# Units of 32 rows in two threads half a unit apart, layer 0 from squares of field sums, MLP in three chunks

## What is computed

```python
# e: (1024, 32, 16) = rows of 32 tables picked by ids
xk = x0 = e
for W in (W0, W1, W2):                     # W0: (32, 32, 64), W1 and W2: (32, 64, 64)
    xk = relu(einsum('bmd,bhd,mhk->bkd', x0, xk, W))
    outs.append(sum(xk, axis=2))           # 64 features of each layer
h = concatenate([concatenate(outs, 1), dense_ctx], 1)        # 208 features
h = maximum(h @ W_top1 + b_top1, 0); h = maximum(h @ W_top2 + b_top2, 0)
y = h @ W_top3
```

## Time and profile before

| | us |
|---|---|
| median of 3 runs (671.03 to 674.77) | 673.65 |
| the profiled execution | 669.01 |
| its span, first to last instruction | 667.2 |

### The profile page before, as it was taken

The page is one execution under the profiler, slowest core; times in us unless marked ns, Lnnn a source line. Parts: engine busy times, 40 slices in busy tenths (PEclk is TensorE's granted clock), DMA queues, the critical chain, the costliest instruction groups (busy, mean ns, idle before and its releaser), DMA issues.

```text
span 667.2 us, 7015 instructions
## 1 busy us (share of the span) xinstructions
PE 588.9 (88%) x2524; PEld 184.4 (28%) x2524; DVE 560.8 (84%) x419; ACT 235.8 (35%) x401; POOL 486.1 (73%) x364
## 2 busy tenths in 40 slices
PE   2558898989899997989899998989898998999998
PEld 1512232222222232322232222323222222323333
DVE  0048998999898998989899998999899989989620
ACT  1030707152441607153341607061432517070513
POOL 6776487877878787877878787887878787858420
PEclk9989898999999898999999999999999999999999
DMA  4398895968869494968969494959779594956000
GB/s 109 95 386 270 325 368 185 344 248 286 332 197 387 146 371 165 353 240 272 346 187 392 162 379 171 365 202 334 286 237 381 167 394 164 397 181 239 0 0 1
DMA packets 82709, 167.95 MB, mean 252 GB/s; under 512 B 38177, under 2 KB 43297, under 8 KB 82674
## 3 DMA queue, kind: packets, MB, share of 16 engines
q1 hardware_dynamic: 74482, 165.39, 68.9%
q0 software_dynamic: 8192, 2.11, 2.3%
HBM read 164.05 MB, written 3.41 MB: 251 GB/s over the span
## 4 chain that ended last, share of the span: by engine, by line
DMA 41%; DVE 18%; SPq 14%; PE 13%; issue 7%; POOL 5%; ACT 2%; ACTq 0%; DVEq 0%
DMA x_rot<-x_rows 20%; DMA x_rows<-gathered 15%; SPq L261 13%; DVE dve_ring L498 10%; PE acc L588 8%; DVE l_tiles L528 5%; POOL gathered L358 4%; DMA x_wide<-x_rows 4%; DVE z_half L512 2%; PE x_ps L613 2%; ACT x_rot_ps L407 2%; SPq L252 1%; DMA gathered<-in_table,idx 1%; PE x_rot_ps L606 1%; PE x_rot_ps L607 1%
## 5 line engine op out<-in xcount | busy, mean ns | idle before, releaser
L498 DVE TENSOR_TENSOR dve_ring<-x_wide,x_ps 128x1024 f32<-128x1024 f32 (+1 forms) x329 | 460.6, 1475 | 11.2 <-ACT x_ps L422 11.2
L588 PE MATMUL acc<-dve_ring,w_sb 128*64 128x512 f32 x1640 | 385.0, 599 | 17.1 <-DVE dve_ring L498 16.2
L383 POOL TENSOR_TENSOR pool_ring<-x_wide,x_sb 128x1024 f32<-128x1024 f32 x102 | 241.7, 2378 | 78.0 <-PE acc L588 45.1
L358 POOL DMA_INDIRECT gathered<-in_table,idx x256 | 243.2, 950 | 72.1 <-issue 69.5
L588 PEld LDWEIGHTS acc<-dve_ring,w_sb 128*64 128x64 f32 x1640 | 110.7, 137 | 275.1 <-issue 147.7
L560 PE MATMUL acc<-l_tiles,w_sb 128*64 128x512 f32 x256 | 76.0, 696 | 37.0 <-DVE l_tiles L528 36.1
L588 PE MATMUL acc<-pool_ring,w_sb 128*64 128x512 f32 x408 | 104.8, 592 | 0.0
L407 ACT COPY x_rot_ps<-x_rot 128x1024 f32<-128x1024 f32 x16 | 16.3, 1016 | 209.5 <-DMA x_rot<-x_rows 209.5
L422 ACT ACTIVATE x_ps<-acc 64x512 f32<-64x512 f32 x128 | 73.1, 571 | 38.7 <-PE acc L564 22.5
L528 DVE TENSOR_TENSOR l_tiles<-x_wide,x_rot_ps 128x1024 f32<-128x1024 f32 x32 | 38.8, 1218 | 56.2 <-ACT x_rot_ps L407 29.2
L431 ACT COPY x_sb<-layer_out 64x512 f32<-64x512 f32 x128 | 79.0, 617 | 3.4
(11 more groups left out here) (28 smaller groups left out, 54.6 us busy)
## 6 DMA issues: line engine op xcount, KB each, us to landing
x_wide<-x_rows SPq DMA_DIRECT2D x256, 512.0 KB, 11.8
l_tiles<-x_rows SPq DMA_DIRECT2D x32, 512.0 KB, 9.3
x_rot<-x_rows SPq DMA_DIRECT2D x16, 512.0 KB
gathered<-in_table,idx POOLq DMA_INDIRECT x256, 2.3
x_rows<-gathered SPq DMA_DIRECT2D x15, 128.0 KB
x_rows<-gathered SPq DMA_DIRECT2D x15, 80.0 KB
w_sb<-in_w SPq DMA_DIRECT2D x2, 512.0 KB, 3.7
x_wide<-in_W_top SPq DMA_DIRECT2D x1, 512.0 KB, 6.7
```

The source lines that it names most:

```text
L358: pool.indirect_dma_start(gathered[:, p % 2, i * DIM:(i + 1) * DIM], None, table, bass.IndirectOffsetOnAxis(ap=idx[:, p, i:i + 1], axis=0) ...
L383: nc.gpsimd.tensor_tensor(pool_ring[:, slot, :], x0_step(p, layer, t), x_sb[layer - 1][:], ALU.mult).then_inc(pool_made, 1)
L498: nc.vector.tensor_tensor(dve_ring[:, slot:slot + width, :], x0_step(p, layer, t, width).rearrange("p (s n) -> p s n", n=WIDE), x_ps[layer ...
L588: last = nc.tensor.matmul(a[c * HK:(c + 1) * HK, :], w_sb[layer - 1][:, step_at(layer, t), :], tile[:, c * CHUNK:(c + 1) * CHUNK], start=( ...
```

## The change

A unit is now 32 rows, 512 columns. There are 32 of them in two threads: thread `c` has units (c, 0) to (c, 15) and owns output half `c` of PE, of `acc[j % 2]` and of `layer_out`. Five functions write each engine's order down from slots. A unit takes 37: layer 1 in slots 0 to 15, layer 0 of the thread's next unit in 16 to 20, layer 2 in 21 to 36. Thread 1 begins 16 slots behind thread 0. So PE's pair of matmuls in a slot is one of each thread, mostly in different layers.

Layer 0 changes its arithmetic. For a pair of fields 2ab = (a+b)^2 - a^2 - b^2. Per unit four matmuls of 32 input rows and 128 outputs (`sums`, L603) sum pairs of fields into four PSUM banks, one matmul on each 32 rows of the array. ACT squares the sums in two instructions of 1,024 columns (L480, L482) and the fields in one of 512 (L484). PE contracts four tiles of squares (L615) and the fields' own (L617), whose weights are corrected once at the start. DVE has no part in it any more, and `x0_rot`, `l0_tiles` and their loads are gone.

DVE works on doubles (two steps of 512 columns, the 1,024 of a step before) or two doubles at once; POOL on doubles, 84 in all in place of 102 steps. `finish` writes half as many columns per unit. There are 512 step loads of 256 KB in place of 304 loads of 512 KB, and 8 gathers per unit. The MLP takes chunks of 512, 384 and 128 rows; the first two stand between the last units' steps on PE, and each has its own output DMA.

```diff
+THREADS = 2
+ROWS = 32
+UNITS = BATCH // (THREADS * ROWS)
+UNIT_SLOTS = 2 * STEPS + L0_STEPS
+DELTA = 16
+L2_SLOT = STEPS + L0_STEPS
+LEAD = 6
+MLP_CHUNKS = ((0, 512), (512, 384), (896, 128))
...
+def pool_doubles(c, j, layer):
+    if j == 0 and layer == 1:
+        return ()
+    if j + AHEAD >= UNITS:
+        return {1: (3, 6), 2: (3, 7)}[layer]
+    return {1: (6,), 2: ((3, 7), (5,))[c]}[layer]
...
+def pe_order():
...
+            works += [(at + i, "step", c, j, 1, i) for i in range(STEPS)]
+            works += [(at + L2_SLOT + i, "step", c, j, 2, i) for i in range(STEPS)]
...
+            works.append((sum_slot(c, j) + 0.5, "sums", c, j + 1, 0, 0))
+            works += [(l0_slot(c, j) + i, "layer0", c, j + 1, 0, i) for i in range(L0_STEPS)]
...
+        works += [(at + i - LEAD, "product", c, j, 1, i, width) for i, width in dve_groups(c, j, 1)]
+        works += [(max(at + L2_SLOT + i - LEAD, at + STEPS + 2.5 + i / 100), "product", c, j, 2, i, width)
...
-            for p in range(PAIRS):
-                contract(p, 1)
-                if p + 1 < PAIRS:
-                    layer0(p + 1)
...
+            def sums(c, j):
+                n = sum_number(c, j)
+                wait_first_step(pe, c, j)
+                if n:
+                    pe.wait_ge(squares_made, 3 * n)
...
+                for q in range(SUM_TILES):
+                    to = x_ps[:, bank + q, :] if q < 2 else sums_ps[:, q - 2, :]
+                    rows = slice(q * FIELDS, (q + 1) * FIELDS)
+                    nc.tensor.matmul(to, in_pair_sb[rows, :], x0_step(c, j, 1, 0)[rows, :],
+                                     start=True, stop=True).then_inc(sums_made, 1)
...
+            def squares(c, j):
+                n = sum_number(c, j)
+                act.wait_ge(sums_made, 4 * (n + 1))
...
+                nc.scalar.activation(pair_squares[:, c, 2:4, :], sums_ps[:], ACT.Square).then_inc(squares_made, 1)
+                wait_first_step(act, c, j)
+                nc.scalar.activation(own_squares[:, c, :], x0_step(c, j, 1, 0), ACT.Square,
```

More of the change, by code:

```diff
@@ L67, in l0_order @@
[L67 to L88, removed]
@@ L91, in ring_slot, with begin, sum_slot @@
-def ring_slot(steps, ring, p, layer, i):
-    return (made_before(steps, p, layer) + i) % ring
-def dve_groups(p, layer):
-    groups = []
[L97 to L100, removed]
+def begin(c, j):
+    return DELTA * c + UNIT_SLOTS * j
+def sum_slot(c, j):
+    if j < 0:
+        return begin(c, 0) - 6
+    return begin(c, j) + (4 if j > 0 else (20, 10)[c])
@@ new lines, in z_slot, with act_order @@
+def z_slot(layer, tile):
+    j = 2 * tile + 1
+    return {0: evac0_slot(1, j - 1) + 4, 1: begin(1, j) + STEPS + 5, 2: begin(1, j + 1) + 2}[layer]
+def act_order():
+    works = []
+    for c, j in [(c, -1) for c in range(THREADS)] + units():
+        at = begin(c, j)
+        if j >= 0:
+            works.append((at + STEPS, "finish", 1, c, j))
+            works.append((at + UNIT_SLOTS, "finish", 2, c, j))
+        if j + 1 < UNITS:
+            works.append((sum_slot(c, j) + 1.5, "squares", 0, c, j + 1))
+            works.append((evac0_slot(c, j), "finish", 0, c, j + 1))
+    works += [(z_slot(layer, tile) + 1, "place", layer, tile, 0) for layer in range(LAYERS) for tile in range(TILES)]
+    for n, first in enumerate((begin(0, UNITS - 1) + STEPS, begin(1, UNITS - 1) + STEPS, begin(1, UNITS) + 3.5)):
+        works += [(first + 1.5 * i + 1.7, "mlp", n, i, 0) for i in range(len(MLP_PARTS))]
+    return in_order(works)
@@ new lines, in sp_order @@
+def sp_order():
+    works = []
+    for c, j in units():
+        at = begin(c, j)
+        if j + 1 < UNITS:
+            works.append((at + 22, "block", c, j + 1, 2))
+            works.append((at + 26, "block", c, j + 1, 3))
+        if j + 2 < UNITS:
+            works.append((at + 28, "stage", c, j + 2, 0))
+            works.append((at + 30, "block", c, j + 2, 0))
+            works.append((at + 34, "block", c, j + 2, 1))
+    works.append((begin(1, UNITS - 2) + UNIT_SLOTS, "mlp", 0, 0, 0))
+    return in_order(works)
@@ L145, in cin_tower @@
[L145 to L151, removed]
+        acc = [psum(f"acc{i}", [P, COLS]) for i in range(2)]
+        sums_ps = psum("sums_ps", [P, 2, COLS])
+        x_ps = psum("x_ps", [P, 4, COLS])
@@ L216, in block_slot @@
[L216 to L231, removed]
@@ L246, in _ @@
         def _(sp):
[L247 to L257, removed]
@@ L419, in finish @@
                 if layer < 2:
[L420 to L423 removed]
+                    for half in range(2):
+                        nc.scalar.activation(x_ps[out_half(half), BANK[layer + 1, c], :], a[out_half(c), :],
+                                             ACT.Relu).then_inc(x_ps_made[layer + 1][c], 1)
```

785 lines of the change are left out of this document (396 added, 389 removed).

## The result

| kernel | median us (range) | ratio to before, 95% | profiled span |
|---|---|---|---|
| before | 673.36 (671.03 to 674.77) | 1 | 667.2 |
| changed | 1536.98 (1535.81 to 1538.12) | 2.291 (2.2815 to 2.3005) | 1536.3 |

The forecast was 654 us, its range 643 to 696. The kernel is slower, and by far more than any rival allowed.

A forecast was written before the change was run, and what follows sets the result against it. DVE was taken to bound the kernel before, PE after the change. Start 64, middle 494.2 (period 34.6), last units 77.4 and tail 12 make 647.6 us of span; with 6.4 to the median 654 us, range 643 to 696.

The forecast's parts named there:

- the paragraph on DMA: Step loads: 512 of 256 KB for 304 of 512 KB, issued 11 or more slots before use; nothing counted.
- 159.8 + 14.28 * P: Whole kernel's time in us for a period P, one unit of each thread; forecast P 34.6 us.
- late loads: Rival at each `sums`: staging and block 0 come 2 us late, all of PE waits; P = 38, 702 us; chance 0.06.
- Work counts: DVE's instructions counted from the order: about 515 us busy in all, products no longer than 1.2 and 2.3 us.
- Price of sums: PE's two new blocks per period: four matmuls side by side 0.86 us, splits 0.35, so 1.2 us a block; period 34.1.
- serial sums: Rival on PE: the four matmuls of `sums` run one after another, 3.43 + 0.35 us a block; 721 us; chance 0.07.
- strict order: Rival on PE: no matmul starts before the one written ahead; 2.9 us a block, P = 37.5, 695 us; chance 0.10.
- Joints, 0.5 us: Handovers between PE, ACT and DVE around layer 0: mostly covered by stock, 0.5 us added per period, making 34.6 us.
- the two engines hold each other up: Rival: DVE waits for PE's ring slots, PE for products; PE gets 95%, P = 35.9, 672 us; chance 0.15.
- Start: Start of the kernel: first product at 31.2 us, 15 us sooner, and slot 26 ends at 64 us.
- Last units and tail: End of the kernel: last units 77.4 us by PE with MLP chunks between steps, then a tail of 12 us.
- From span to median, 6.4 us: Added to the forecast span of 647.6 us, as the median of the runs lies 6.4 us over the profiled span.

The follow-up runs named there:

- e1: Changed kernel with the two outer dimensions of the step loads' source exchanged (32 fields outermost, then 4 quarters), weights reordered to match; 695.32 us, ratio 1.034.
- e11: e9 with one load for each block of four steps, 128 partitions of 8 KB, in place of four of 2 KB; 649.23 us, ratio 0.966.
- e5: e1 with all of DVE's products two steps wide, none of four; 664.11 us, ratio 0.989.
- e15: e11 with DVE's products of four steps put back; 684.49 us, ratio 1.020.
- e9: e5 with the MLP's weights loaded 10.5 slots earlier; 660.26 us, ratio 0.981.

## Where the prediction failed

**The step that failed is the paragraph on DMA**: "The share of 0.77 to 0.79 may stay, with smaller rows at a worse rate" and "I count nothing here". I read sizes and counts of the loads, and not the order of the dimensions in `load_step`. What I put at nothing cost 842 us of the 883 between forecast and result, by e1. With the order of the dimensions read, the rows give the price: 276 GB/s at a share of 0.79 are 21.8 for each engine, four engines move 87 GB/s, and a period loads 32 * 0.262 = 8.4 MB: 96 us. With 159.8 + 14.28 * P that is 1,531 us. That this comes so near to 1,537 is luck: the period was 90.2 us, which gives 1,448, and the start and the end, which the formula keeps as they were, took some 90 us more. The rival "late loads" named the right place and the right victim (SP serves two threads in one line, PE's wait blocks both), but it was priced as a delay of 2 us, not as a rate.

The other steps are read from e1 and e11, where the loads are spread:

- *Work counts*: right. DVE 516.3 us for 515 in the changed kernel; products last 1.21 and 2.29 us as before.
- *Price of sums*: right. The passes start at 214.31, 214.84, and in e11 a period without any wait is 34.20 us, for 34.1 by count. A block costs 1.17 us for 1.2 (in e11 204.13 to 205.73 from the last pass start before it to the first behind it, less 0.43); 0.31 of that is the change of split, where my own rows add up to 0.3 and I wrote 0.35. Four matmuls on different input rows run side by side; serial sums and strict order fall.
- *Joints, 0.5 us*: the term that was too small. e1's period is 36.8 for 34.6. From slot 26 to slot 555 (the first step behind the last layer 0 product) it took 528.5 us (71.7 to 600.2) for 494.2: 34.3 us too much. I had seen the two engines hold each other up as a rival at P = 35.9 and chance 0.15; once the loads are spread it was the true case, and stronger. I weighed it by how full the engines are; what decided was how long one instruction waits and works (four slots, 2.3 us) with another thread's need behind it. e5 removes most of it (34.9), e15 with the loads in time brings it back (36.6). What e5 and e9 have over 34.20 is gone in e11, together with PE's waits for loads.
- *Start*: slot 26 at 71.7 us in e1 and 68.8 in e11, for 64. In e1 the first product comes at 33.1 us for 31.2, and behind it DVE waits three times for ring slots, 2.2 to 3.4 us, which I hadn't counted.
- *Last units and tail*: 93.9 us in e1 for 89.4, with a wait of 3.63 us for the MLP's weights, which I had not looked for; 85.7 in e11.
- *From span to median, 6.4 us*: too large. In e11 the median lies 2.0 us over the span. The profiled execution of the kernel before was faster than each of its other runs (669.01 us, the others 671.03 and more).

In e11 the errors of the parts cancel, which is luck: 68.8 + 492.8 + 85.7 = 647.2 us of span, but for rounding, for a forecast of 647.6. And e11 is not the kernel forecast: it has the loads spread and one for a block, products of two steps, and the MLP's weights earlier. With these the plan is worth what the sum said; the changed kernel and e1 didn't carry it out.

## What to carry to other kernels

Read every changed DMA's address pattern from its outermost dimension: a small count there (4 and 8 here) confines the load to as many engines, and the sign in a profile is a flat GB/s line with a low DMA share while everyone waits for loads. When one engine serves two threads in a fixed order, cut its instructions and its demands for buffer space small, even at the cost of more work: here 5 us more of DVE brought 31 us. Where a restructuring comes out far slower than counted, mend the one broken resource first, before giving up the rest.

## What was new about the hardware

- With 4 outermost in its loads' source the kernel moved 94 GB/s over its span, with 8 138, with 32 207 and up to 285 in a fortieth, for the same bytes in rows of the same size. The packets in flight were most often 4, 8 and 16.
- 16 outermost times 8 isn't as good as 32 times 4: packets of 2 KB in 125 ns for 84, with 16 in flight in both. And packets of 8 KB took 601 ns in loads of 32 partitions, 309 in loads of 128.
- Four fp32 matmuls of 32 input rows and 512 columns, on four groups of input rows, start together, all eight passes within 0.55 us of starts (e1, e11); the block costs 1.17 us with the change of split before and behind.
